# GpSimd takes one fill in eight of a state-space scan: a lent turn in the second layer's first half

## The reference

```python
delta = jax.nn.softplus(jnp.einsum('blr,er->ble', dt, dt_w) + dt_b)
A = -jnp.exp(A_log)
dA = jnp.exp(delta[..., None] * A)
dBu = (delta * xc)[..., None] * Bm[:, :, None, :]

def step(h, t):
    dA_t, dBu_t, C_t = t
    h = dA_t * h + dBu_t
    return (h, jnp.einsum('ben,bn->be', h, C_t))
```

## Time and profile before

| | |
|---|---|
| median of three executions | 3130.73 us |
| the profiled execution, its own time | 3137.26 us |
| its span | 3135.9 us |
| VectorE busy in the span | 2335.6 us (74%) |
| GpSimd busy in the span | 1623.4 us (52%) |
| ScalarE busy in the span | 1882.8 us (60%) |
| first scan of the second layer | at 721.0 us |
| first item of the fifth unit | at 1022.1 us |
| last product of GpSimd in the layer ends | at 1784.2 us |

### The profile page before, as it was taken

The page is one execution under the profiler, slowest core; times in us unless marked ns, Lnnn a source line. Parts: engine busy times, 40 slices in busy tenths (PEclk is TensorE's granted clock), DMA queues, the critical chain, the costliest instruction groups (busy, mean ns, idle before and its releaser), DMA issues.

```text
span 3135.9 us, 40110 instructions
## 1 busy us (share of the span) xinstructions
PE 2709.0 (86%) x14665; PEld 1172.3 (37%) x14738; DVE 2335.6 (74%) x2621; ACT 1882.8 (60%) x3556; POOL 1623.4 (52%) x993
## 2 busy tenths in 40 slices
PE   6699998986668898889988588889986899999996
PEld 3133333442222332333333154323322555555553
DVE  3888873538999999999999633367784788888883
ACT  3366666135447767777777443177773666777774
POOL 3121210123588888887887810245564655666562
PEclk6799999996678999988889699889998999999998
DMA  4123110021113222221222110011110110111110
GB/s 108 32 45 51 34 33 2 0 69 49 29 41 68 44 46 46 60 59 35 44 50 49 46 79 1 1 27 27 27 27 12 25 24 14 25 25 25 25 25 28
DMA packets 79730, 114.29 MB, mean 36 GB/s; under 512 B 16271, under 2 KB 49423, under 8 KB 78107
## 3 DMA queue, kind: packets, MB, share of 16 engines
q1 hardware_dynamic: 68268, 103.06, 13.7%
q0 software_dynamic: 11264, 8.66, 2.1%
HBM read 37.69 MB, written 17.33 MB: 18 GB/s over the span
## 4 chain that ended last, share of the span: by engine, by line
PE 51%; DVE 26%; ACT 10%; issue 7%; POOL 3%; DMA 1%; POOLq 0%; DVEq 0%; SPq 0%; another core or an unknown queue 0%; ACTq 0%
DVE layer_mamba_state L1422 12%; DVE psum L1411 7%; PE psum L1190 3%; PE psum L2711 3%; PE psum L1280 3%; PE psum L834 3%; PE psum L2774 2%; PE psum L2744 2%; DVE layer_peak L775 2%; PE psum L2270 2%; PE psum L2725 2%; PE psum L2785 2%; PE psum L965 2%; PE psum L814 2%; ACT layer_mamba_decay L1363 2%
## 5 line engine op out<-in xcount | busy, mean ns | idle before, releaser
L1458 POOL TENSOR_TENSOR layer_mamba_state<-layer_mamba_state,layer_mamba_c 128x1024 f32<-128x1024 f32 x320 | 781.5, 2487 | 229.6 <-DVE layer_mamba_state L1422 225.0
L1422 DVE TENSOR_TENSOR_SCAN layer_mamba_state<-layer_mamba_decay,psum 128x1024 f32<-128x1024 f32 x320 | 731.4, 2286 | 35.9 <-DVE psum L1411 0.5
L1280 PE MATMUL psum<-layer_mamba_state,two_to_one 128*64 128x512 f32 x1280 | 404.5, 715 | 14.1 <-POOL layer_mamba_state L1458 14.0
L775 DVE TENSOR_REDUCE layer_peak<-psum 128x2 f32<-128x1024 f32 x256 | 308.3, 1220 | 73.0 <-PE psum L746 68.4
L848 ACT ACTIVATE layer_exps<-psum 128x1024 f32<-128x1024 f32 x256 | 256.0, 1023 | 153.9 <-PE psum L814 153.9
L142 ACT ACT_TABLE_LOAD x172 | 220.7, 1283 | 78.3 <-DVE layer_stats L3035 25.9
L1363 ACT ACTIVATE layer_mamba_decay<-layer_mamba_delta_wide,layer_weights 128x511 f32<-128x511 f32 x384 | 251.3, 712 | 24.1 <-DMA layer_mamba_delta_wide<-layer_mamba_delta 14.5
L1411 DVE TENSOR_TENSOR psum<-psum,layer_mamba_u_wide 128x1024 f32<-128x1024 f32 x192 | 236.3, 1231 | 21.9 <-DMA layer_mamba_u_wide<-layer_mamba_work 9.3
L3107 POOL TENSOR_TENSOR layer_qk<-layer_qk,layer_v_between 128x1024 f32<-128x1024 f32 x64 | 151.0, 2359 | 145.0 <-DVE layer_v_between L3009 143.0
L1373 ACT ACTIVATE layer_mamba_c<-psum 128x512 f32<-128x512 f32 x192 | 113.2, 589 | 157.3 <-PE psum L1238 155.3
L2913 ACT ACTIVATE layer_p<-psum,layer_stats 128x128 f32<-128x128 f32 x512 | 181.7, 386 | 38.5 <-issue 21.7
(11 more groups left out here) (359 smaller groups left out, 5765.6 us busy)
## 6 DMA issues: line engine op xcount, KB each, us to landing
layer_mamba_delta_wide<-layer_mamba_delta SPq DMA_DIRECT2D x96, 128.0 KB, 2.3
layer_mamba_u_wide<-layer_mamba_work SPq DMA_DIRECT2D x96, 128.0 KB, 2.3
attn<-layer_mamba_delta SPq DMA_DIRECT2D x64, 128.0 KB
attn<-layer_mamba_work SPq DMA_DIRECT2D x64, 128.0 KB
layer_v_between<-layer_v SPq DMA_DIRECT2D x16, 512.0 KB, 4.4
qk_dram<-layer_qk_parts SPq DMA_DIRECT2D x16, 384.0 KB, 3.0
layer_q_rows<-qk_dram SPq DMA_DIRECT2D x96, 64.0 KB
layer_k_rows<-qk_dram SPq DMA_DIRECT2D x96, 64.0 KB
```

Of the source, the lines that this page charges most:

```text
L775: dve.tensor_reduce(self.peak[s][:, block, 2 * g:2 * g + 2], c.psum[:, at:at + 2, :], AX.X, ALU.max).then_inc(self.maxed, 1)
L1280: e = pe.matmul(c.psum[j * HALF:(j + 1) * HALF, self.sum_banks[h], :], c.two_to_one[:, :], self.state[i % len(self.state)][:, j, :], start ...
L1422: dve.tensor_tensor_scan(state, decay, self.fill.rearrange("p j t -> p (j t)"), 0.0, ALU.mult, ALU.add).then_inc(self.scanned, 1)
L1458: pool.tensor_tensor(state, state, self.both(self.c_wide[turn % self.C_BUFFERS][:, :]), ALU.mult).then_inc(self.multiplied, 1)
```

## The change

In a lent turn (turn 2 of each unit, from the fifth unit on: 12 turns, 24 items) VectorE makes no fill. In its place:

- TensorE spreads B earlier (`pe_lent`), and ScalarE copies it from PSUM to SBUF (`act_lent`), into a buffer that the lists of experts used before (`in_block`, seen as f32).
- GpSimd multiplies `u_wide` by this copy, straight into the state buffer of the item (`pool_fills`).
- The scan then reads decay and fill from SBUF, and writes over the fill.

The 16 score products stand in four groups of four with a time each, and the plan's numbers are new.

```diff
+    def is_lent(self, turn):
+        return turn % TURNS in self.plan.lent and turn >= self.plan.lent_from * TURNS
...
-        return merged(self.pe_b(), self.pe_c())
+        return merged(self.pe_b(), self.pe_c(), self.pe_lent())
...
+    def pe_lent(self):
+        c, hold, plan = self.c, self.c.pe_hold, self.plan
+        for turn in range(self.units * TURNS):
+            unit, m = divmod(turn, TURNS)
+            if self.is_lent(turn):
+                now = plan.turn(turn) + plan.lent_spread
+                yield now
+                hold.wait_ge(self.set_up, self.all_set_up)
+                hold.wait_ge(self.bc_split, unit + 1)
+                at = self.banks.take(("b", turn), now, plan.turn(turn) + plan.lent_copy + 0.7)
+                c.wait_bank(at)
+                self.pe_spread(at, unit % 2, 2 * m).then_inc(self.lent_spread, 1)
+                c.bank_read[at] = self.b_copied, self.lent_before(turn + 1)
...
+    def act_lent(self):
+        act, hold = self.c.act, self.c.act_hold
+        for turn in range(self.units * TURNS):
+            if self.is_lent(turn):
+                n = self.lent_before(turn)
+                yield self.plan.turn(turn) + self.plan.lent_copy
+                hold.wait_ge(*self.b_wide_free)
+                hold.wait_ge(self.lent_spread, n + 1)
+                for lent_filled in self.lent_filled:
+                    hold.wait_ge(lent_filled, n)
+                act.activation(self.b_wide, self.bank(("b", turn)), ACT.Copy).then_inc(self.b_copied, 1)
...
     def dve_fills(self):
         dve, hold = self.c.dve, self.c.dve_hold
         for turn, h, i, now in self.items(self.plan.FILL):
+            if self.is_lent(turn):
+                continue
             yield now
...
-            hold.wait_ge(self.filled, i + 1)
-            dve.tensor_tensor_scan(state, decay, self.fill.rearrange("p j t -> p (j t)"), 0.0, ALU.mult, ALU.add).then_inc(
-                self.scanned, 1)
+            if self.is_lent(turn):
+                fill = state
+                hold.wait_ge(self.lent_filled[h], self.lent_before(turn) + 1)
+            else:
+                fill = self.fill.rearrange("p j t -> p (j t)")
+                hold.wait_ge(self.filled, self.fills(turn, h))
+            dve.tensor_tensor_scan(state, decay, fill, 0.0, ALU.mult, ALU.add).then_inc(self.scanned, 1)
...
-        return merged(self.pool_products(), self.pool_inputs())
+        return merged(self.pool_products(), self.pool_inputs(), self.pool_fills())
+
+    def pool_fills(self):
+        pool, hold = self.c.pool, self.c.pool_hold
+        for turn in range(self.units * TURNS):
+            if self.is_lent(turn):
+                unit, n = turn // TURNS, self.lent_before(turn)
+                for h in range(self.halves):
+                    yield self.plan.turn(turn) + self.plan.lent_fill[h]
+                    hold.wait_ge(self.b_copied, n + 1)
+                    hold.wait_ge(self.u_ready[h], self.transferred(unit))
+                    i = turn * self.halves + h
+                    hold.wait_ge(self.summed, i + 1 - len(self.state))
+                    pool.tensor_tensor(self.state[i % len(self.state)][:, :, :], self.u_wide[unit % self.wides][h][:, :, :],
+                                       self.both(self.b_wide), ALU.mult).then_inc(self.lent_filled[h], 1)
...
 PLAN1 = MambaPlan(
-    start=48.0, pace=8.3, item=4.34, first=0.55, spread=-6.72, c_spread=-4.36, copy=-2.12, decay=-5.86,
...
+    start=48.0, pace=8.3, item=4.22, first=0.97, spread=-7.03, c_spread=-4.26, copy=-2.12, decay=-6.45,
...
+    multiply=6.16, sum=15.81, gate=1.5, back=2.16, out=2.48, lent=(2,), lent_from=4, lent_spread=-9.27, lent_copy=-7.72,
+    lent_fill=(-7.18, -3.22))
...
+SCORES_AT = [0.0, 0.1, 0.2, -2.18]
```

63 lines of the change are left out of this document (42 added, 21 removed).

## The result

The changed kernel takes 3176.63 us (median; 3159.65 to 3188.55) where the kernel before, run beside it, took 3131.19. The ratio is 1.0141, with a 95% interval of 1.0094 to 1.0189: **45 us slower, where +13 was forecast**, and outside the range. The profiled execution of the changed kernel is its slowest, 3188.55 us, so the traces differ by 51.3 us.

What follows compares the result with a forecast made beforehand. VectorE was taken as the bound, with GpSimd becoming it from the fifth unit after the change. GpSimd's shortfall of +16 and the start's -3 gave +13 us: 3144 us against the median, range 3108 to 3168.

Steps and rivals of the forecast that it cites:

- Fills off VectorE, -32.6: VectorE, 24 lent items: each falls from 3.75 to 2.39 us without its fill, saving 32.6 us if nothing waits.
- GpSimd's account, and with it the +16: GpSimd from the fifth unit: 108.2 us asked of 92.4 fillable, short by 15.8, so it becomes the bound: +16 us.
- The lock holds for scans with two SBUF inputs: Lent scans: they and GpSimd instructions reading SBUF share a lock held for the whole instruction; all 24 are hit.
- Its price for VectorE, 39.6 us: Lent scans on VectorE: waits of 1.1 us for a pair's first, 2.2 for its second, 39.6 over 12 pairs.
- rival A: Lent scans: the lock hardly bites, second scans go free at indirect DMAs; -8 to -25 us, about 3112; chance 0.22 (two forms).
- rival C: Lent turns: late fills on top, first scans wait 2.2 us too; +30 to +40 us, about 3165; chance 0.18.
- What it costs GpSimd: GpSimd during lent scans: it stands still 2.15 us in each of 24, 51.6 us in all.
- the wait would then be nothing: Lent scans beside a running indirect DMA: no wait, so a pair's 3.3 us would be 1.1 to 2.2.
- The lock's +7 lies inside, not beside.: From the fifth unit: VectorE's loss of 7 us (39.6 against 32.6) is contained in GpSimd's +16, not added.
- Start, -3: Layer's start: the first unit's products follow the score products at once, 3.9 us earlier; -3 us, between 0 and -3.9.
- The other moved numbers: nothing, within 2 us either way.: Rest of the new plan: a DMA or product shifts by one place, costing nothing, within 2 us either way.
- ScalarE's 12 copies: nothing: ScalarE in lent turns: 12 more copies of 0.59 us, 7 us beside 219 us idle, with 2 to 3 us to spare.

Runs made afterwards that it cites:

- the run with the old plan: The kernel before, its plan and lists of planned times kept, with the lent turns added at the change's own offsets: 3158.62 us, ratio 1.0080.
- unread fills: Changed kernel, lent scans reading an older PSUM fill, GpSimd's 24 fills going to a BF16 buffer nobody reads and no scan waiting for them: 3139.88 us, ratio 1.0024.
- the plan alone: The changed kernel with its new plan but no lent turn, VectorE making all 256 fills: 3142.01 us, ratio 1.0028.
- fills twice: Changed kernel, VectorE making all fills and scanning from the bank, GpSimd making its 24 too, unread but waited for by the scans: 3156.18 us, ratio 1.0071.

## Why the prediction was wrong, point by point

The runs give the sum of the change: the plan +9; VectorE without 24 fills -31; GpSimd's load +37; the second SBUF input +29. They come to the measured +44 because each is the difference of one run and the next, and this says nothing for them: taken in another order they have other sizes (the load +13 with VectorE's fills left to it, the second input +47 in the kernel before). The first three are uncertain by some 3 to 10 us, the last by 16.

- *Fills off VectorE, -32.6.* Right: -31.
- *GpSimd's account, and with it the +16.* **This is the step that failed.** I added up what GpSimd was asked for (108.2) and what it could fill (92.4), and let only the difference, 15.8 us, reach VectorE: "GpSimd becomes the bound". It did not become one, it kept 72 us of idle time, and the loss was larger. An account of totals holds where work can move; here each engine keeps its row. A fill pushes the products behind it back by 2.4 us at once, TensorE stands at their sums, and what stands behind comes late to VectorE, however much idle time GpSimd has later. With no scan waiting for a fill, where the account has nothing to charge (56.6 asked of 92.4; without the lock I had allowed 8 us, for late fills and the tail), the load cost 30 us, and 18 of these (11 in the profiled executions) went when the sums moved one item back.
- *The lock holds for scans with two SBUF inputs.* Right in kind: 13 of the 24 took over 2.3 us, up to 9.14, and with the input in PSUM (the run with the scans from the bank) all took 2.26. The Trainium skill, page "SBUF — State Buffer", section "Who interferes with whom", names this contention for a VectorE instruction with two SBUF inputs beside a GpSimd one that reads SBUF; the trace agrees.
- *Its price for VectorE, 39.6 us.* The stretch was 33.6, but otherwise shared out: 2.3 us for the first of a pair, not 1.1, and 0.5 for the second, not 2.2. I said that between two back-to-back scans the waiting product gets in, from one place in the earlier trace rows. The eight second scans that stood right behind the first took 2.26 us each, but that does not speak against the reading: at none of these eight places was a product waiting. At seven GpSimd was in an indirect add when the second scan began, as rival A had it, and in unit 15 its next product came after. Where one did wait, once, in the run with the old plan, it got in and the second scan took 4.37 us. So the step was right and its frequency wrong. The 5.9 us belong to three of the four scans that had first waited for a late fill. Those met the product that had gone ahead meanwhile, as rival C had it.
- *"What it costs GpSimd", 51.6 us.* GpSimd's busy time in the window grew by 82.3 us (641.5 to 723.8), 25.7 beyond the fills' 56.6: half. And of these the adds have 23.7 (95.1 to 118.8).
- *An indirect DMA beside such a scan: "the wait would then be nothing".* Right for the scan's wait: nine lent scans began while an add ran, and eight took 2.26 or 2.27 us (the ninth, 5.19, was caught by the product next in GpSimd's row). The other direction is wrong: adds were held up by the scan, 3.4 us for 1.58. The section on the hardware has the numbers.
- *"The lock's +7 lies inside, not beside."* Not borne out: taking the second SBUF input away left +15 of the +44. How the two combine otherwise is open, as the sizes change with the order in which they are taken.
- *Start, -3.* Right within the spread. The two traces compared above differ by 7.3, but the one of before is the longest of its kind: from the score products to the first scan it took 41.8 to 46.3 us in the four executions with the old front, and 39.0 to 40.9 in the fourteen with the new one, 4 us less in the mean.
- *"The other moved numbers: nothing, within 2 us either way."* Wrong by 9 us: the plan's loss in units 1 and 2 eats its start. I looked at the order at the lent turns alone.
- *ScalarE's 12 copies: nothing.* Their own time is hidden, but the copy is late with the spread that it reads, and GpSimd waited 22 us for it in 3 waits. Whether that is TensorE's row again is open: with the sums moved it fell to 9.8 us in the change, but stayed at 14.3 for 15.0 with the unread fills.

Of the rivals C was nearest: slower by 30 to 40 with fills 3 to 5 us late. Four fills were late, by 3.9 us each, 15.5 us; that is a part, and the run with earlier fills, which all but took them away, was no faster, with other waits in their place. Rival A's own terms give -7 to -19 us, not -8 to -25; nothing else hangs on that.

## What to carry to other kernels

When work moves to an engine with idle time, the idle total says little: look whom the delayed instructions release, what stands behind those waits in the next engine's row, and shift that row together with the move (here one item of slack for the sums gave back some 17 of 44 us). Check the form of the consumer too: a scan that reads both inputs from SBUF paid 1.4 us each and held GpSimd's DMAs, and the same scan with one input in PSUM paid nothing.

## What the runs showed of the hardware that was not expected

**A VectorE scan with two SBUF inputs holds up GpSimd's indirect DMAs.** Mean of the 60 adds in the window: 1.59 us before; 1.58 in the runs with no scan of this kind, however much load GpSimd had (the plan alone, no fills, unread fills, fills twice, scans from the bank); 1.77 with 12 such scans; 1.98 with 24 (1.95 to 1.99 in the runs that vary the change), and 2.07 (123.9 us in 60) in the run with the second SBUF input alone. A held one takes 3.4 us (11 of the 60 in the changed kernel; those that no such scan overlapped took at most 1.63). In unit 6 one ended 1.4 us after the first scan of the pair, under the second, which did not hold it. The Trainium skill, page "SBUF — State Buffer", section "Who interferes with whom", infers from the interfaces that an instruction which only reads through the shared pair leaves descriptor generation alone; the measurement speaks against that for this form.

**GpSimd keeps the lock over several instructions that stand back to back; for VectorE that is not shown.** The longest lent scan, at 1777.86 us, timeline of VectorE, then of GpSimd:

```profile
1777.86 11.32 DVE L1474 TENSOR_TENSOR_SCAN layer_mamba_state<-layer_mamba_decay,layer_mamba_state 128x1024 f32<-128x1024 f32 x2
```

```profile
1777.28 2.95 POOL L1503 TENSOR_TENSOR layer_mamba_state<-attn,layer_in_block 128x1024 f32<-128x1024 f32 x1
1779.59 5.25 POOL L1523 TENSOR_TENSOR layer_mamba_state<-layer_mamba_state,layer_mamba_c 128x1024 f32<-128x1024 f32 x2
1787.14 4.18 POOL L1523 TENSOR_TENSOR layer_mamba_state<-layer_mamba_state,layer_mamba_c 128x1024 f32<-128x1024 f32 x1 [2.30 <-DVE layer_mamba_state L1474]
```

The first scan of the two waited for a fill and two products, to 1784.84, and ran in the gap behind them (9.14 us in all); the second followed at once in 2.26 us, and the product that starts at 1787.14 was held until it was over (4.18 us for 2.36). Five of the first scans of a pair (units 10, 11, 13, 14, 15) waited for two or three GpSimd instructions in a row, and came in at a gap or at a DMA.

Two scans of VectorE in a row held nothing out in this trace, for no product waited between them. Unit 14 of the run with the old plan has one that did, timeline of VectorE, then of GpSimd:

```profile
1688.70 6.55 DVE L1474 TENSOR_TENSOR_SCAN layer_mamba_state<-layer_mamba_decay,layer_mamba_state 128x1024 f32<-128x1024 f32 x2
```

```profile
1689.51 3.60 POOL L1523 TENSOR_TENSOR layer_mamba_state<-layer_mamba_state,layer_mamba_c 128x1024 f32<-128x1024 f32 x1
```

The first scan took 2.27 us, to 1690.97. Then the product ran, to 1693.11, and the second scan took 4.37 us, 2.15 of them behind it. So here the waiting engine came in between two instructions back to back, as between L1981 and L1983 in the earlier trace rows.
